# A Flamingo-style double layer on one core: every operation's place in its engine's order set group by group

## The reference, cut to what matters

```python
x = x + tanh(g_xattn[0]) * L0_xattn(layernorm(x), ctx)   # q, rope, 8 heads over 128 keys, softmax, Wout
x = x + tanh(g_ffn[0])   * L0_ffn(layernorm(x))          # ternary w_fc (+ low rank), relu squared, ternary w_proj
x = x + tanh(g_xattn[1]) * L1_xattn(layernorm(x), ctx)   # x W1^T + mean(ctx W2^T) + b
x = x + tanh(g_ffn[1])   * L1_ffn(layernorm(x))          # rmsnorm, 8-bit rounding, ternary w1, gelu, the same, w2
```

## Time and profile before

| | us |
|---|---|
| median of 3 runs | 1346.24 |
| lowest, highest | 1342.7, 1351.59 |
| span of the profiled execution | 1340.0 |
| PE busy in it | 1135.0 |
| DVE, ACT, POOL busy | 974.3, 788.0, 597.8 |

### The profile page before, as it was taken

The page is one execution under the profiler, slowest core; times in us unless marked ns, Lnnn a source line. Parts: engine busy times, 40 slices in busy tenths (PEclk is TensorE's granted clock), DMA queues, the critical chain, the costliest instruction groups (busy, mean ns, idle before and its releaser), DMA issues.

```text
span 1340.0 us, 19939 instructions
## 1 busy us (share of the span) xinstructions
PE 1135.0 (85%) x7092; PEld 695.2 (52%) x7380; DVE 974.3 (73%) x2017; ACT 788.0 (59%) x1509; POOL 597.8 (45%) x569
## 2 busy tenths in 40 slices
PE   4353777989898999999999999999999988899975
PEld 3332545546374646555564747464656556475621
DVE  3895587887758676877778686868687776877574
ACT  2455773839465574838384656657483838475523
POOL 1221254645534535455463555454545435363430
PEclk9666898999999999999999999999999999999997
DMA  6957744353423444443635343444444343524132
GB/s 220 298 179 214 238 135 97 78 111 71 91 67 84 98 87 100 87 97 81 130 79 100 70 87 77 96 98 87 99 87 87 87 99 74 114 55 86 24 67 51
DMA packets 302241, 140.28 MB, mean 105 GB/s; under 512 B 258096, under 2 KB 276016, under 8 KB 300464
## 3 DMA queue, kind: packets, MB, share of 16 engines
q1 hardware_dynamic: 299840, 136.62, 44.4%
q10 hardware_dynamic: 2304, 2.40, 0.6%
HBM read 57.97 MB, written 9.18 MB: 50 GB/s over the span
## 4 chain that ended last, share of the span: by engine, by line
DVE 27%; PE 27%; ACT 21%; POOL 12%; issue 9%; DMA 3%; SPq 1%; DVEq 0%; POOLq 0%; ACTq 0%
ACT e L882 6%; PE ps L1693 5%; PE ps L1645 5%; PE ps L1629 4%; DVE st L1256 4%; PE ps L1551 3%; PE ps L1596 3%; ACT rl L920 3%; POOL rs L649 2%; DVE amax L986 2%; ACT hid L925 2%; ACT sq L931 2%; POOL hid L674 2%; POOL e L679 2%; POOL r L692 2%
## 5 line engine op out<-in xcount | busy, mean ns | idle before, releaser
L1629 PE MATMUL ps<-xT,fcT 128*128 128x256 f16 x2048 | 261.1, 275 | 1.9 <-DVE scbc L1240 1.0
L1645 PE MATMUL ps<-pjT,hid 128*128 128x512 fp8e4 x1024 | 239.4, 385 | 24.1 <-POOL hid L674 22.0
L649 POOL TENSOR_TENSOR rs<-ve,nhalf 128x1 f32<-128x1 f32 x160 | 100.6, 629 | 289.1 <-DVE ve L1261 220.0
L1629 PEld LDWEIGHTS ps<-xT,fcT 128*128 128x128 fp8e4 x2048 | 201.0, 99 | 33.7 <-ACT rl L920 4.3
L674 POOL TENSOR_TENSOR hid<-sq,hid 128x512 f16<-128x512 f32 x128 | 163.0, 1280 | 101.8 <-ACT sq L931 101.8
L1645 PEld LDWEIGHTS ps<-pjT,hid 128*128 128x128 f16 x1024 | 98.5, 99 | 100.8 <-issue 4.9
L1693 PE MATMUL ps<-w2T,hT 128*128 128x512 fp8e4 x512 | 130.1, 413 | 12.5 <-DMA hT<-q 12.5
L1681 PE MATMUL ps<-w1T,q4T 128*128 128x512 fp8e4 x512 | 127.9, 390 | 15.0 <-DMA q4T<-x16b 6.5
L920 ACT ACTIVATE rl<-ps,rsf 128x256 f32<-128x256 f32 x256 | 106.6, 470 | 38.4 <-PE ps L1633 38.2
L679 POOL TENSOR_TENSOR e<-e,einv 128x512 f32<-128x512 f32 x64 | 73.1, 1142 | 125.7 <-DVE einv L1303 116.1
L882 ACT ACTIVATE e<-ps,nmb,sig 128x128 f32<-128x128 f32 x256 | 113.0, 455 | 13.3 <-DVE nmb L1299 13.0
(11 more groups left out here) (202 smaller groups left out, 2112.1 us busy)
## 6 DMA issues: line engine op xcount, KB each, us to landing
qS<-qT SPq DMA_DIRECT2D x128, 64.0 KB, 2.1
...
```

Source lines behind the costliest of these rows:

```text
L649: pool.tensor_tensor(rs[:, n, t:t + 1], ve[:, n, t:t + 1], nhalf[:, :], ALU.pow).then_inc(done, 1)
L1629: pe.matmul(dst, fcT[:, k, f * P:(f + 1) * P], xT2[:, xs, k, :], start=(xs == 0 and k == 0), stop=False)
L1645: mm = pe.matmul(ps[:, FFN0 + t, :], hid[:, xs, c, t * P:(t + 1) * P], pjT[:, c, :], start=(c == 0 and xs == 0), stop=(c == FC - 1 and xs ...
```

## The change

`AT` and `OWN` go. In their place `ORDER` has for every engine and operation one row for each of the 16 groups, and the numbers in it are the operation's index in that engine's whole order. `PREP` gets indices of the same kind. The operations, their buffers, their semaphores and their waits stay as they are. Orders differ on all engines: of PE's 641 entries 539 stand at another index. Below are the core of the removed tables, PE's new rows as far as they are used further on, and two of the new preparation tables; the other engines' rows are of the same form.

```diff
-        AT = dict(
-            PE=dict(up=(195289, 200771, 211516, 211832, 213196, 215372, 223295, 232242),
-                    down=(234779, 239752, 240173, 240395, 246633, 255546, 255658, 258146), q=(134222, 134477),
-                    s=(148339, 150714, 151017, 158017), pv=(180977, 181748), wo=(187448, 187515), low=(194115,),
-                    wx=(258176, 279737), w1=(297817, 297968, 297972, 302716, 303110, 305014, 307920, 314686),
-                    w2=(320266, 329143)),
...
-        OWN = dict(
-            PE={0: dict(up=(205266, 208022, 213864, 215912, 218783, 222988, 227978, 228019),
-                    down=(231226, 232524, 234274, 236935, 235949, 236798, 244093, 252184), q=(137786, 154679),
-                    s=(155271, 155707, 159745, 163080), pv=(181108, 186102), wo=(194698, 195386), low=(199579,),
-                    wx=(261678, 275465), w1=(281396, 285562, 285626, 293091, 294621, 295879, 310141, 317635),
-                    w2=(319929, 325214)),
...
+        ORDER = dict(
+            PE=dict(
+                up=((30, 31, 32, 33, 35, 38, 39, 40), (59, 60, 61, 62, 64, 65, 71, 72),
+                    (98, 99, 105, 107, 108, 111, 112, 114), (139, 141, 144, 145, 148, 154, 155, 156),
+                    (174, 175, 176, 178, 180, 183, 188, 190), (212, 214, 215, 216, 218, 219, 220, 221),
+                    (251, 254, 255, 256, 258, 261, 266, 267), (293, 295, 298, 300, 301, 309, 310, 312),
+                    (332, 333, 335, 338, 340, 341, 342, 350), (370, 371, 373, 374, 379, 380, 383, 386),
+                    (408, 409, 411, 412, 414, 417, 420, 423), (448, 449, 450, 452, 456, 460, 463, 464),
+                    (488, 489, 493, 494, 496, 497, 504, 505), (523, 524, 528, 529, 531, 534, 537, 538),
+                    (566, 568, 571, 573, 574, 580, 581, 584), (601, 602, 605, 608, 609, 612, 613, 618)),
+                down=((42, 43, 44, 47, 45, 46, 48, 51), (77, 78, 79, 83, 82, 88, 90, 91),
+                      (115, 116, 117, 123, 125, 126, 128, 129), (157, 158, 159, 161, 160, 164, 165, 168),
+                      (192, 193, 194, 197, 201, 202, 204, 205), (225, 228, 229, 230, 231, 232, 233, 234),
+                      (270, 271, 272, 279, 282, 283, 285, 286), (314, 317, 318, 319, 316, 322, 323, 324),
+                      (352, 353, 354, 357, 358, 361, 362, 364), (387, 388, 389, 394, 391, 400, 401, 402),
+                      (426, 427, 428, 431, 436, 439, 440, 442), (467, 471, 472, 474, 468, 478, 479, 480),
+                      (508, 509, 510, 511, 514, 515, 518, 519), (548, 549, 550, 551, 542, 553, 555, 556),
+                      (586, 587, 588, 592, 591, 595, 596, 597), (619, 621, 622, 623, 620, 625, 626, 627)),
+                q=((6, 7), (27, 28), (57, 58), (93, 94), (133, 134), (172, 173), (211, 213), (250, 252), (288, 289),
+                   (327, 328), (366, 367), (406, 407), (444, 445), (483, 484), (525, 526), (561, 562)),
+                s=((9, 10, 11, 12), (34, 36, 37, 41), (63, 66, 67, 68), (97, 101, 102, 104), (140, 142, 143, 146),
+                   (179, 181, 182, 184), (222, 223, 224, 227), (257, 259, 260, 262), (294, 296, 297, 299),
+                   (334, 336, 337, 339), (372, 375, 376, 377), (413, 415, 416, 418), (451, 453, 454, 457),
+                   (490, 491, 492, 495), (530, 532, 533, 535), (567, 569, 570, 572)),
+                pv=((20, 21), (49, 50), (80, 81), (119, 122), (162, 163), (195, 196), (239, 244), (275, 278),
+                    (313, 315), (355, 356), (392, 393), (432, 433), (469, 470), (512, 513), (552, 554), (589, 590)),
+                wo=((24, 25), (52, 53), (84, 85), (124, 127), (166, 167), (199, 200), (246, 247), (280, 281),
+                    (320, 321), (359, 360), (395, 396), (437, 438), (473, 475), (516, 517), (557, 558), (593, 594)),
+                low=((29,), (56,), (96,), (135,), (171,), (209,), (249,), (291,), (329,), (368,), (405,), (446,),
+                     (485,), (522,), (564,), (600,)),
+                wx=((54, 55), (92, 106), (131, 138), (170, 187), (210, 226), (245, 263), (287, 292), (326, 331),
+                    (365, 378), (404, 419), (443, 455), (482, 486), (521, 536), (560, 565), (599, 603), (628, 630)),
+                w1=((69, 70, 73, 74, 75, 76, 86, 87), (100, 103, 109, 110, 113, 118, 120, 121),
+                    (136, 137, 147, 149, 150, 151, 152, 153), (185, 186, 189, 191, 198, 203, 206, 207),
+                    (235, 236, 237, 238, 240, 241, 242, 243), (264, 265, 268, 269, 273, 274, 276, 277),
+                    (302, 303, 304, 305, 306, 307, 308, 311), (343, 344, 345, 346, 347, 348, 349, 351),
+                    (381, 382, 384, 385, 390, 397, 398, 399), (421, 422, 424, 425, 429, 430, 434, 435),
+                    (458, 459, 461, 462, 465, 466, 476, 477), (498, 499, 500, 501, 502, 503, 506, 507),
+                    (539, 540, 541, 543, 544, 545, 546, 547), (575, 576, 577, 578, 579, 582, 583, 585),
+                    (606, 607, 610, 611, 614, 615, 616, 617), (631, 632, 633, 634, 635, 636, 637, 638)),
+                w2=((89, 95), (130, 132), (169, 177), (208, 217), (248, 253), (284, 290), (325, 330), (363, 369),
+                    (403, 410), (441, 447), (481, 487), (520, 527), (559, 563), (598, 604), (624, 629), (639, 640))),
+            DVE=dict(
...
         PREP = dict(
...
-            POOL=dict(rot_k=(102685, 103653), wq_max=(91104,), kv_max=(109256,), csb=(147525,), wo_max=(136688,),
-                    low_zero=(126778,), bound=(150790,), wx_max=(163451,), above=(0, 0, 0, 0, 0, 0, 0, 0)),
-            SP=dict(ctx=(60431,), wk=(62486,), wq=(60882,), wv=(64936,),
-                    piece=(64310, 96899, 76370, 129192, 131996, 112166, 142384, 150134, 160255, 156057, 179110, 179066, 180702, 179178, 180704, 199937, 203741, 203796, 207638, 214385, 224552, 239662, 241831, 267762),
-                    wo=(62510,), wc=(111205,), wx=(86250,), b1=(152082,), k_pair=(132753,)))
+            POOL=dict(rot_k=(4, 7), wq_max=(0,), kv_max=(8,), csb=(3,), wo_max=(9,), low_zero=(12,), bound=(18,),
+                      wx_max=(15,), above=(0, 0, 0, 0, 0, 0, 0, 0)),
+            SP=dict(ctx=(1,), wk=(2,), wq=(0,), wv=(5,),
+                    piece=(7, 8, 10, 15, 16, 18, 19, 22, 25, 26, 29, 32, 36, 28, 31, 37, 40, 41, 45, 47, 49, 51, 52, 55),
+                    wo=(4,), wc=(3,), wx=(6,), b1=(17,), k_pair=(20,)))
         placed = {}
-        for eng, tables in AT.items():
-            for name, places in tables.items():
-                for g in range(GROUPS):
-                    own = OWN[eng].get(g)
-                    for k, p in enumerate(own[name] if own else places):
-                        placed.setdefault((eng, name, p if own else p + g * SLOTS), []).append((k, g))
+        for eng, tables in ORDER.items():
+            for name, rows in tables.items():
+                for g, places in enumerate(rows):
+                    for k, p in enumerate(places):
+                        placed.setdefault((eng, name, p), []).append((k, g))
```

More of the change, by code:

```diff
@@ L299, in build @@
-        PREP = dict(
[L300 to L316, removed]
-            POOL=dict(rot_k=(102685, 103653), wq_max=(91104,), kv_max=(109256,), csb=(147525,), wo_max=(136688,),
-                    low_zero=(126778,), bound=(150790,), wx_max=(163451,), above=(0, 0, 0, 0, 0, 0, 0, 0)),
-            SP=dict(ctx=(60431,), wk=(62486,), wq=(60882,), wv=(64936,),
-                    piece=(64310, 96899, 76370, 129192, 131996, 112166, 142384, 150134, 160255, 156057, 179110, 179066, 180702, 179178, 180704, 199937, 203741, 203796, 207638, 214385, 224552, 239662, 241831, 267762),
-                    wo=(62510,), wc=(111205,), wx=(86250,), b1=(152082,), k_pair=(132753,)))
@@ new lines, in build @@
+        PREP = dict(
+            PE=dict(k=(0, 1), v=(2, 3), low=(4,), mix=(8,), tern=(5, 13, 14, 15, 16, 17, 18, 23), low_t=(19,),
+                    row_scale=(22,), mean=(26,)),
+            DVE=dict(const=(0,), ctx_sum=(4,), rot_k=(9, 11), wq_max=(1,), wq_scale=(5,), k_max=(12,), wq_lo=(6,),
+                     v_max=(13,), kv_scale=(18,), k_lo=(21,), v_lo=(28, 29), signs=(15, 20, 27, 49, 50, 53, 56, 64),
+                     thr=(14, 19, 22, 36, 37, 38, 43, 60), wo_max=(10,), v_top=(16,), wo_scale=(24,), k_other=(35,),
+                     wo_lo=(32,), mix_row=(63,), low_rank=(47,), v_parts=(59,), wx_max=(17,), hidden=(57,),
+                     wx_scale=(41,), wx_lo=(66,), row_scale=(67,), mean=(74,), k_now=(34,), diag=(65,),
+                     round=(76, 79, 84, 90, 92, 97, 99, 111), clip=(81, 82, 89, 93, 96, 106, 109, 116)),
+            ACT=dict(wq=(0,), k_hi=(7,), v_hi=(8, 9), tanh=(4,), wo=(10,), kv_save=(16,),
+                     evac=(20, 24, 27, 29, 31, 34, 39, 44), rows=(3, 5, 6, 12, 14, 15, 17, 26), low=(40,), wx=(28,),
+                     sums=(30, 32, 38, 41, 45, 46, 47, 48), lift=(51, 52, 56, 60, 62, 74, 77, 81)),
```

(2 more changed lines are left out.)

241 lines of the change are left out of this document (128 added, 113 removed), and 42 rows, old and new, of tables (exp, h, hid, max).

## The result

The changed kernel takes 1272.32 us (median of 4 runs, 1270.21 to 1275.72) against 1344.47 us before on the same chip: a ratio of 0.946, interval 0.942 to 0.949, faster by 72 us. The forecast was 1295 in a range of 1248 to 1332, 51 us faster. Sign and range held; 21 us of gain were not foreseen. Of these, 15 are in the spans, which fell by 66.1 us. The other 6 come from which executions were profiled. The 6.2 us by which the median before stood above the profiled span, and which the prediction carried over, are not start-up and completion: in every execution for which both are given the time is 1.75 to 1.87 us above the span, and the rest is spread between executions. The profiled execution of the changed kernel is the slowest of its four.

What follows compares the result with a forecast made beforehand. Bound by TensorE, busy 1135 of 1340.0 us, with waits and lowered clock costing the middle 102.3 us. Middle minus 34, head minus 17, tail 0 give a 1289.0 span, plus 6.2 carried over: 1295 us, range 1248 to 1332.

Steps and rivals of the forecast that it cites:

- First `up`, 29.4 to 6: Between low-rank product and first up: other products cover PE's wait for `tlow`, which falls from 29.4 to 6 us.
- small waits: PE's remaining idle time in the middle, outside the three named waits: 17.0 us before, 12 kept in the forecast.
- `qS` ahead of `wo`, 9.1 to 0: Between second p times v and output projection: a longer cover removes PE's 9.1 us wait.
- ACT's phase, 25 us of waits where `hid`'s 22 were: Ups and exponentials: ACT needs about 31 us per group, PE's cover is often shorter; 25 us of waits, bounds 0 to 80.
- Covers that become short, 10 us: Ahead of the low-rank product, first score and w2 in groups 3, 4 and 6: new lateness, 10 us, from 5 to 25.
- Clock, 24.8 to 15: Middle's fifteen stretches: loss to PE's lowered clock falls from 24.8 to 15 us, from 0 to 25 either way.
- Head, minus 17: Before the first low-rank product: earlier w_fc piece and `wx_max` all-reduce save 17 us, from 0 to minus 35.
- Tail, 0: After the last low-rank product: one chain in both orders, no change, from minus 6 to plus 6 us.
- Hand-ordered pitch (67.2): Rival, chance 0.22: all fifteen middle pitches come to the 67.2 us of the stretch at 1166.3; time 1252 us.
- Waits only move: Rival, chance 0.10: the middle's 34 us of gain all come back as other waits, head gives 5; 1341 us.
- Slower by ACT's phase: Rival, chance 0.08: from first up to `down` piece 3 ACT takes 36.5 us per group instead of 31; 1367 us.
- the rule on shared SBUF interfaces: GpSimd and VectorE collide, costing about 1 us per group where POOL stands on PE's path, 15 in all; 1310 us.

Runs made afterwards that it cites:

- e2_nocover: Changed kernel with the first up directly behind the low-rank product again in groups 1 to 14, nothing else moved: 1298.97 us.
- e1_cover: Kernel before, with the second w2 tile between the low-rank product and the first up on PE in groups 3 to 13: 1335.01 us, ratio 0.992.
- e5_qcover: Kernel before, with the next group's first q product between the low-rank product and the first up in groups 3 to 14: 1403.59 us, ratio 1.046.
- e8_qfeed: Kernel before, next group's first q ahead of the first up in groups 3 to 12, its DVE, ACT, POOL and SP feeders moved earlier too: 1358.76 us, ratio 1.010.
- e7_after_act: Changed kernel with one extra, unread ACTIVATE on ACT for each unit of the first layer: 1315.72 us.
- e3_newhead: Every engine's new order up to the first low-rank product, the order of the kernel before behind it: 1315.89 us, ratio 0.978.
- e3b_oldhead: Old orders up to the first low-rank product, the changed kernel's behind it, with group 1's q in its head: 1297.43 us, ratio 0.964.

## Why the prediction was right, and where its sizes were off

*First `up`, 29.4 to 6:* right, 4.9: group 13 waited 2.0 and group 15 2.9, as counted, and group 2, counted at 1.6, not at all. Group 0, which the sum left out, waited 2.9 at 139 us. `e2_nocover` shows what the step is worth in place, 26.6 us. Not foreseen is that the same step is worth 9.5 in the old pattern, where the cover comes before its data. The prediction counted lengths of covers, and the new orders of SP, DVE, ACT and POOL, which bring the data in ahead of them, it took for granted. That these are part of the gain `e1_cover`, `e5_qcover` and `e8_qfeed` show by what happens when they don't fit; the reverse was not tried. The sum's start was also off: it gave every pitch 65.5 us of work, but the one from 148.7 has PE busy 56.4 with 368 matmuls. So it had 77.5 us of idle time in the middle and 17.0 in small waits, where the rows have 94.1 and, beside the three named waits, 33.6.

*`qS` ahead of `wo`, 9.1 to 0:* right, 1.2.

*ACT's phase, 25 us of waits where `hid`'s 22 were:* the step that failed, in size. 31 us were summed for the phase and only 26 are needed. Group 11, the one with the shortest cover (25.9 us), on ACT:

```profile
906.57 0.84 ACT L984 ACTIVATE rl<-ps,rsf 128x256 f32<-128x256 f32 x2 [4.83 <-PE ps L1697]
...
913.84 0.46 ACT L946 ACTIVATE e<-ps,nmb,sig 128x128 f32<-128x128 f32 x1
914.20 0.19 ACT L946 ACTIVATION_READ_ACCUMULATOR e<-ps,nmb,sig 128x1 f32 x1
914.29 0.45 ACT L946 ACTIVATE e<-ps,nmb,sig 128x128 f32<-128x128 f32 x1
...
931.99 0.61 ACT L995 ACTIVATE sq<-rl 128x512 f32<-128x512 f32 x1
```

From the first relu at 906.57 to the end of the last square at 932.60 are 26.0 us, with all four softmax units and the table load inside. The rows overlap: the next exponential starts 0.45 us after the last, though its own 0.46 and the accumulator's 0.19 follow one another in the list. The sum added the 3.2 us of reads and every other overlap in full, 30.6 in all. With 26.0, covers of 25.9 to 38.7 suffice, and the waits are 3.2 (`rl`) and 0 (`hid`). The forecast of waits in groups 3, 7 and 11 was wrong with it. `e7_after_act` is near the world it had described, a phase some 4 us longer, near 30: there PE idles 37.5 us more, where 25 had been counted from the covers' lack. So the mechanism stands and the margin is thin.

*Covers that become short, 10 us:* too small. Waits for `hT` (+10.0), `qS`'s transpose (+2.5), `xT` (+3.0), and "issue" ahead of `q`, `low` and `down` (+5.5, +1.8, +2.0) add to 25. Together the two terms were forecast at 35 and measured at 28: that they nearly cancel is luck.

*Clock, 24.8 to 15:* the same sum over the fifteen stretches is 13.1; right.

*Work moved between the stretches:* a second size that was off. The prediction gave group 1's `q` to the head's gain and left 65.5 us of work in every pitch of the middle. By busy time less the clock's share the middle's work was 965.9 before and 953.8 after, 12 us less, for a head with 8.9 us more. `e3_newhead` shows this part alone, 9.2 us; where the other 3 are stays open. The middle's minus 54.3 is thus 12 of work, for nothing forecast, 30.6 of idle time, for 24.5, and 11.7 of clock, for 9.8.

*Head, minus 17:* minus 14.6 in its own length. ACT's 20.4 us wait for the piece of w_fc is 5.7 us long in the changed kernel; PE's 19.0 us wait at `ident` is 3.9 in the changed kernel and 17.8 in `e3b_oldhead`. POOL's step went as the prediction had it. Before, the last `norm` stands behind the all-reduce of `wx_max`:

```profile
108.83 0.79 POOL L701 PARTITION_ALL_REDUCE wmaxa<-wmax  x1 [6.92 <-issue]
119.20 1.03 POOL L679 TENSOR_TENSOR e<-e,einv 128x512 f32<-128x512 f32 x1 [9.58 <-issue]
```

In the changed kernel it follows the `norm` before it, 18.5 us earlier:

```profile
99.43 1.03 POOL L743 TENSOR_TENSOR e<-e,einv 128x512 f32<-128x512 f32 x1 [9.40 <-issue]
100.66 1.04 POOL L743 TENSOR_TENSOR e<-e,einv 128x512 f32<-128x512 f32 x1 [0.19 <-DVE einv L1367]
```

The 9.4 us in the first of these rows are another wait, behind the all-reduce of `bound`, and that one was there before too (8.9 us, ahead of 99.87). `pv` of group 0, whose second unit needs the last `norm`, starts at 111.16 for 125.51, 14.4 us earlier, nearly the head's 14.6. Which of the moves brings how much of the head was not tried apart.

*Tail, 0:* plus 2.8.

*The rivals.* Hand-ordered pitch (67.2): the middle came to 68.7 a group, halfway between it and the 70.0 of the forecast, partly by the moved work. Waits only move: true of the one-engine moves of `e1_cover` and `e5_qcover`, not of the change. Slower by ACT's phase: not seen, but `e7_after_act` puts a price on it, 43 us for 4.0 us a group, 11 for each us of phase, near the 13 reckoned. Of the rule on shared SBUF interfaces (the Trainium skill, GPSIMD Engine Reference, section "8. Key points") nothing was seen that cost 15 us: POOL is busy 580.8 us for 597.8 before, with the same 569 instructions. No run tried it by itself.
